# One reciprocal of the softmax row sums for both query tiles of a head pair, in a fused decoder layer on one Trainium2 core

## The reference

```python
x = layernorm(x + self_attention(x))           # 16 query heads, 4 key/value heads, head size 64, rotary, a slope per head
x = layernorm(x + cross_attention(x, ctx))     # 16 heads of 16, windows of 64 keys, masks from cell numbers
x = layernorm(x + ffn(x))                      # ternary weights, quantized activations, silu(gate) * up
```

```python
attn = softmax(q @ k.T / sqrt(64) + slope * (j - i))     # per head: 256 queries x 256 keys
out = attn @ v
```

## Time and profile before

| | us |
|---|---|
| median of 3 runs | 2368.91 (2364.6 to 2370.87) |
| the profiled execution | 2367.9 |
| its span in the trace | 2366.1 |
| PE busy | 2263.7 (96%) |
| DVE busy | 1853.2 (78%) |
| ACT busy | 1565.2 (66%) |
| POOL busy | 1218.5 (51%) |

### The profile page before, as it was taken

One profiled execution on the slowest core, in us unless ns is written; L12 is line 12 of the kernel. 1 busy time (PEld: TensorE's weight loads), 2 busy tenths in 40 slices (PEclk: granted clock), 3 DMA queues, 4 the chain that ended last, 5 costly groups with the idle time before them and its releaser, 6 DMA issues. The chain is left out here.

```text
span 2366.1 us, 53992 instructions
## 1 busy us (share of the span) xinstructions
PE 2263.7 (96%) x17641; PEld 1643.0 (69%) x17706; DVE 1853.2 (78%) x8005; ACT 1565.2 (66%) x4577; POOL 1218.5 (51%) x1422
## 2 busy tenths in 40 slices
PE   5889999999999999999999999999999999999985
PEld 4667677777777777777777777777777777777652
DVE  4868877788877778887778887777888777888855
ACT  2577666677666677666667766667766667776651
POOL 3445555554555555555555555555555555555521
PEclk9999999999999999999999999999999999999996
DMA  4010100111110110110111111011111011010100
GB/s 161 14 38 20 35 22 25 35 31 29 33 34 13 35 34 26 33 35 13 34 35 26 32 35 33 15 35 32 29 33 35 13 35 35 26 32 26 30 10 14
DMA packets 84660, 74.64 MB, mean 32 GB/s; under 512 B 18337, under 2 KB 79137, under 8 KB 84385
## 3 DMA queue, kind: packets, MB, share of 16 engines
q1 hardware_dynamic: 84384, 71.19, 10.9%
HBM read 45.98 MB, written 8.39 MB: 23 GB/s over the span
## 5 line engine op out<-in xcount | busy, mean ns | idle before, releaser
L1151 POOL TENSOR_TENSOR prob<-prob,precs 128x512 f32<-128x512 f32 x512 | 528.3, 1044 | 384.9 <-DVE precs L809 380.9
L1066 ACT ACTIVATE prob<-prob,nmax 128x256 f32<-128x256 f32 x1024 | 508.2, 498 | 227.9 <-DVE nmax L802 227.9
L1073 ACT COPY pT<-bank 128x512 f32<-128x512 f32 x512 | 298.9, 584 | 286.2 <-PE bank L441 280.7
L802 DVE CUSTOM_DVE_ANT_0 prob<-bank,alibi 128x256 f32<-128x256 f32 x1024 | 372.2, 419 | 140.1 <-PE bank L536 139.2
L1089 ACT ACTIVATE px<-px,nmx 128x128 f32<-128x128 f32 x1024 | 313.5, 392 | 73.2 <-DVE nmx L894 73.1
L441 PE MATMUL bank<-ident,prob 128*128 128x128 f32 x2048 | 314.6, 276 | 8.3 <-ACT pT L1073 7.1
L441 PEld LDWEIGHTS bank<-ident,prob 128*128 128x128 f32 x2048 | 238.6, 141 | 96.4 <-issue 55.8
L1142 POOL TENSOR_TENSOR qtok<-qtok,by_sin 128x512 f32<-128x512 f32 x128 | 163.4, 1276 | 255.2 <-DVE by_sin L792 255.0
L536 PE MATMUL bank<-kk,qq 64*128 64x256 f32 x2048 | 291.4, 403 | 0.9 <-DVE nmax L802 0.9
L554 PE MATMUL bank<-pT,v_sb 128*64 128x256 f32 x2048 | 277.6, 392 | 3.2 <-ACT oT L1078 2.4
L894 DVE CUSTOM_DVE_ANT_0 px<-bank,mask 128x128 f32<-128x128 f32 x1024 | 226.1, 286 | 18.4 <-PE bank L610 13.8
(11 more groups left out here) (187 smaller groups left out, 4489.1 us busy)
## 6 DMA issues: line engine op xcount, KB each, us to landing
ctxt<-in_ctx SPq DMA_DIRECT2D x32, 256.0 KB, 2.9
xT<-in_xT SPq DMA_DIRECT2D x32, 256.0 KB, 3.6
cT<-in_ctxT SPq DMA_DIRECT2D x32, 256.0 KB, 2.7
xtok<-in_x SPq DMA_DIRECT2D x32, 256.0 KB, 3.2
kx<-kxT SPq DMA_DIRECT2D x256, 32.0 KB, 2.0
vs<-vx SPq DMA_DIRECT2D x64, 128.0 KB, 2.4
out_y<-y SPq DMA_DIRECT2D x32, 256.0 KB, 2.1
cellk<-in_cell SPq DMA_DIRECT2D x32, 64.0 KB, 3.5
```

The source lines that it names most:

```text
L802: v.tensor_tensor_reduce(out=prob[:, (2 * p + q) % SLOTS, c, :], in0=psum[SCORES[c]][:, q * L:(q + 1) * L], in1=alibi[:, p % 2, c, :], sca ...
L1066: nc.scalar.activation(prob[:, (2 * p + q) % SLOTS, c, :], prob[:, (2 * p + q) % SLOTS, c, :], ACT.Exp, bias=nmax[:, i:i + 1], scale=-1.0, ...
L1073: nc.scalar.copy(pT[:, p % 2, :, :, q * P:(q + 1) * P].rearrange("p c k n -> p (c k) n"), bank[:].rearrange("p (c n) -> p c n", c=4)).then ...
L1151: g.tensor_tensor(prob[:, n % SLOTS, :, :], prob[:, n % SLOTS, :, :], precs[:, 2 * n:2 * n + 2].unsqueeze(2).to_broadcast([P, 2, L]), ALU. ...
```

## The change

On DVE the reciprocal of an even R step now covers four columns, both tiles of the pair, and waits for the last of the pair's four exponentials; the odd R step issues nothing on DVE. POOL still scales each tile at its own R step, and waits for the reciprocal of the pair. The order lists are the same. The count of reciprocals per batch goes from 16 to 8, of POOL's multiplications it stays 16.

```diff
-    S_mm=8, s_neg=32, p_exp=32, p_recip=16, p_norm=16, ...
+    S_mm=8, s_neg=32, p_exp=32, p_recip=8, p_norm=16, ...
@@ DVE
                     elif kind == "R":
                         n, = args
-                        dve.wait_ge(*at("p_exp", b, 2 * n + 1))
-                        v.reciprocal(precs[:, 2 * n:2 * n + 2], psums[:, 2 * n:2 * n + 2]).then_inc(sem["p_recip"], 1)
+                        if n % 2 == 0:
+                            dve.wait_ge(*at("p_exp", b, 2 * n + 3))
+                            v.reciprocal(precs[:, 2 * n:2 * n + 4], psums[:, 2 * n:2 * n + 4]).then_inc(sem["p_recip"], 1)
@@ POOL
-                        pool.wait_ge(*at("p_recip", b, n))
+                        pool.wait_ge(*at("p_recip", b, n // 2))
```

More of the change, by code:

```diff
@@ L44 @@
     x_hi=1, x_lo=1, proj_mm=6, rot_prod=15, rot_sum=5, v_new=1, v_ready=1, kT_mm=1, k_ready=1, qT_mm=4, q_ready=4,
-    S_mm=8, s_neg=32, p_exp=32, p_recip=16, p_norm=16, T_mm=16, pT_ready=16, O_mm=8, oT_ready=8, W_mm=1, y_ready=1,
+    S_mm=8, s_neg=32, p_exp=32, p_recip=8, p_norm=16, T_mm=16, pT_ready=16, O_mm=8, oT_ready=8, W_mm=1, y_ready=1,
     y_st=2, y_mv=2, y_eps=3, y_rstd=1, x1_norm=1, x1_ready=1, NX_mm=1, yT_ready=1, QX_mm=1, qx_prod=1, qx_rot=1, QXT_mm=1, qxT_ready=1,
```

## The result

| | before | after |
|---|---|---|
| median of the runs, us | 2369.3 (4 runs) | 2397.88 (4 runs) |
| span of the profiled execution | 2366.1 | 2393.2 |
| one pass of BODY (median distance of T 0 of successive batches on PE) | 70.03 | 70.81 |
| T 0 of batch 0 to T 0 of batch 4 (HEAD) | 265.9 | 273.4 |
| start of the span to T 0 of batch 0 | 46.6 | 44.0 |

The change makes the kernel slower by 1.22%, ratio 1.0122 with a 95% interval of 1.0104 to 1.0139. The direction was forecast; the size was not: +13.5 us were expected and 28.6 came. The difference of the spans, 27.1 us, divides into 20.3 for the 26 passes between T 0 of batch 4 and of batch 30, 7.5 in HEAD, 1.9 behind, and -2.6 ahead of T 0 of batch 0.

The account below looks back on a forecast made before the run. PE, busy 69.38 of 70.00 us a pass, was taken to bound the kernel. 27 x (0.47 - 0.08) = 10.5 us plus 3 for HEAD and TAIL, on 2367.9, gave 2381 us; range 2367 to 2396.

Parts of the forecast that it names:

- Removed reciprocals: On DVE, 256 of 512 reciprocals go, 20 us of work, off the path except where PE waits for DVE.
- POOL's 380.9 us of waiting: The kernel's largest wait, POOL for reciprocals: idle time of an engine with room, worth nothing by itself.
- 0.98 us of standstill at pairs 1, 3 and 7: DVE's even reciprocal waits for the pair's fourth exponential, 0.98 us each at these pairs; 3.1 us a pass overall.
- Pairs 1 and 7 cost nothing: DVE's later waits for PE, 1.78 and 1.11 us, take up the lateness there; cost 0.
- Pair 3: The place that pays: DVE's lateness behind R 6 reaches PE through xqT, G 0 and G 3; 0.47 us a pass.
- the step that was to cost 0.47 us: G 3's weight load on PE hangs on quarter 2's line 972 on DVE without slack; 0.47 us late each pass.
- rival A: The lateness is hidden because G 3 has unseen room, so no change: 2369 us; chance 0.28.
- R 11 gives back 0.08 us at TX 1 1: Without R 11 in DVE's run ending in SX 2's evacuation, PE's 0.5 us wait before TX 1 1 shrinks by 0.08.
- The sum of the body: Over 27 passes, 0.47 us lost less 0.08 us gained each: 10.5 us.
- Rival B: All 0.98 us of pair 3's standstill reaches PE because DVE's holes don't absorb: 29 us more, 2397 us; chance 0.10.
- HEAD and TAIL: 3 us: Three even tiles in HEAD, among them T 0 of batch 1, pass lateness to PE: 3 us, bounds 0 and 20.
- the two rules: Grouping saves about 60 ns per DVE instruction, time at or below 2368 us; breaking up may finish sooner, so change slows.

Follow-up runs that it names:

- e8: Kernel before with one merged reciprocal only for pairs 2, 4, 5 and 6; median 2370.35 us, ratio 1.0011, pass 70.01 us.
- e11: Kernel before with merged reciprocals in batches 4 to 30 and step R 6 placed behind XQ and YS in BODY; 2368.31 us, ratio 1.0007.
- e2: Kernel before with merged reciprocals for all pairs but pair 3; 2375.72 us, ratio 1.0033, pass 70.02 us.
- e4: Changed kernel with PE's transposes XQ in PSUM bank 6 in place of 7; 2389.84 us, ratio 1.0097, pass 70.47 us.
- e7: Changed kernel with step R 6 placed behind XQ and YS in BODY; 2377.54 us, ratio 1.0046, pass 70.03 us.
- e1: Kernel before with a merged reciprocal for pair 3 only; 2392.21 us, ratio 1.0096, pass 70.85 us.
- e3: Kernel before, reciprocals unmerged, but tile 6's waits for its pair's fourth exponential; 2390.33 us, ratio 1.0092, pass 70.84 us.
- e9: Kernel before with merged reciprocals only in batches 0 to 3; 2377.31 us, ratio 1.0039, HEAD 273.6 us.
- e5: Kernel before with PE's transposes XQ in PSUM bank 6 in place of 7; 2367.7 us, ratio 1.0003.
- e6: Kernel before, reciprocals unmerged, but tile 6's waits for its pair's third exponential; 2377.93 us, ratio 1.0037, pass 70.36 us.
- e10: Kernel before with merged reciprocals only in batches 4 to 30; 2392.95 us, ratio 1.0103, pass 70.93 us.

## Why the prediction was right in its direction and short in its size

- *Removed reciprocals are worth next to nothing; POOL's 380.9 us of waiting is worth nothing.* Right (e8, e11), though DVE's busy time fell by 12 us, not by the 20 named. POOL now waits 419.0 us for reciprocals, 38 more than before, and PE doesn't wait for a scaled tile in the body.
- *0.98 us of standstill at pairs 1, 3 and 7.* Right: waits of 1.1, 1.1 and 1.0 us in the trace.
- *Pairs 1 and 7 cost nothing.* Right (e2).
- *Pair 3: "G 0 comes some 0.3 us late; PE's wait of 0.37 us before QX takes up part".* Here it failed. I asked who reads xqT and found G 0; I did not ask whose bank the line for xqT frees. NX stands ahead of G 0 on PE, needs bank 7 and had 0.14 us of room, so the lateness reached PE as 0.84 us, at once, and the 0.37 us could not absorb it, since yT depends on NX. With PE 0.80 late, the tanh of quarter 1 was too, DVE waited 0.16 us for it, and at G 3 DVE was no later than PE: the step that was to cost 0.47 us added nothing in the changed kernel. The direction came from the standstill at pair 3, which was right, and not from the path behind it. e4 removes the shared bank, and that path appears nearly as it was worked out, 0.46 us at G 3. The wait on line 972, which the prediction brought up against rival A as G 3's, was G 2's; that G 3 has no slack rested on the 0.05 us alone, and e4 bears it out.
- *R 11 gives back 0.08 us at TX 1 1.* Mis-sized: 0.03 us there in the kernels that merge pair 5 (0.80 to 0.77 late in the changed kernel, and the same step in e2, e7 and e8), and nothing in e1 and e3, where R 11 stands.
- *The sum of the body.* 27 x 0.39 = 10.5 was expected; 0.78 a pass was measured, 20.3 us over 26 passes. Rival B had 24 for the body, 5 for HEAD and TAIL, and 2397 in all, which is next to the 2397.88 measured, but by luck: QX's wait did move along with PE, yet for a reason B does not name, the wait at NX ahead of it, and B's body was too large and its HEAD too small.
- *HEAD and TAIL: 3 us.* HEAD alone lost 7.5 (e9). T 0 of batch 1 waited 0.76 us for POOL and waits 1.75 now:

```profile
109.65 0.42 PEld L441 LDWEIGHTS bank<-ident,prob 128*128 128x128 f32 x4 [1.75 <-POOL prob L1152]
```

  That term of 1 us was as said; but along HEAD the lateness of PE rises in some ten places by 0.3 to 1.1 us each, at cross-attention scores and their transposes, at attention tiles, at a G, and I had counted three. Which DVE wait stands behind each was not traced one by one, so the cause of HEAD's loss is shown only as far as its own merged pairs (e9). HEAD came out at 264.5 to 267.2 us in kernels that merge no pair there (e5, e6, e10, e11), and 7.5 is clear of that.

The Trainium skill, Perfetto Trace Analysis, "Optimization Strategy", says that a bubble which repeats for a stretch on the engine that should be saturated can mean that PSUM or SBUF is short. The trace agrees: the new wait comes 27 times, once a pass, 16.5 us in PE's records, and is gone when XQ has another bank (e4); but the bank was shared before too, at no cost (e5), and only the late emptying made it short. Of the two rules that the prediction took from the Trainium skill, Perfetto Trace Analysis, "Optimizing Scalar/DVE Operations", the one on breaking instructions up gave the direction: 12 us less DVE work came with 28 us more time. What counted was the wait that the merge brings and not the number of instructions (e3).

## What to carry to other kernels

An operation that is merged waits for the last of its inputs, and in an in-order queue everything behind it waits too: price the merge by that wait at each place where it is issued, not by the instruction saved. To find who feels it, follow every semaphore that the delayed instructions raise, the ones that free a PSUM bank or a buffer as well as the ones that say that data is ready; the consumer that is hurt first may not read the data at all. Here the wait landed on a path with 0.14 us of room, and placing the merged instruction two steps later removed it at no cost (e7).

## What the runs showed of the hardware

A reciprocal of four columns lasts 177 ns, one of two 156, in the same kernel otherwise; at R 6 the next DVE instruction starts 0.09 us behind its start in place of 0.08. PE passed a late start on almost one to one: 0.49 and 0.98 us of DVE standstill became 0.35 and 0.84 us at NX. Apart from the 0.14 us of room, PE's queue took up 0.04 us between NX and G 0, and then nothing for the rest of the pass (e3: 0.80 at G 0, 0.80 at its end; e6: 0.30 and 0.31). PE's weight load of G 3 started 0.05 us behind the end of the DVE record that freed its bank, in the kernel before, the changed one and e4.
